# One audio tower on one core: a deeper step in the attention stage, a 32-bit pointwise convolution and a new order of work in the token stage

## The chip, the core and the metric

The kernel runs on one core of a Trainium2 chip. The time is the device time of one execution in microseconds. The kernel before took 2148.81 us (median of three runs, 2148.19 to 2150.49). One execution was also recorded by the hardware profiler. The engines of the core are PE (TensorE: matmuls, with the weight loads listed apart as PEld), DVE (VectorE), ACT (ScalarE), POOL (GpSimd) and SP (SyncE, which here only issues DMAs).

## The reference

Three stages follow each other, each on the result of the one before. All numbers are float32.

```
x [16, 64, 2048]
token stage, per batch b of 16:
  h  = conv1d(x, 7 taps, 64 -> 128 channels)              # [128, 2048]
  h  = gelu(groupnorm(h))                                 # mean and variance over channels and time
  h  = depthwise conv(h, 5 taps, stride 2) + bias         # [128, 1024]
  h  = pointwise conv(h)           # a 128 x 128 matrix product
  h  = gelu(groupnorm(h))                                 # [128, 1024]: 128 tokens of 1024 features
attention stage, on layernorm(h), 32 heads:
  q_c = rmsnorm(h @ w_qa)   [128, 384];  k_c = rmsnorm((h @ w_kva)[:, :128]);  k_r = rope(the other 64)
  scores = (q_nope . k_nope + rope(q_rope) . k_r) * 192**-0.5;  softmax over the 128 keys of the batch
  h += concat over heads(softmax @ v) @ w_o
last stage: h += layernorm(h) @ W_base.T + bias + two of eight low-rank experts per token
```

## The kernel before, in words

Nearly every matrix product is computed in 16 bits: an operand is multiplied by a power of two and stored as a high half (an ACT copy to float16) and a low half (a DVE instruction that subtracts the high half from the scaled source). Three matmuls, high by high, low by high and high by low, add up in PSUM. `dw_h` and `dw_l` are such a pair, made of `dw`, the result of the depthwise convolution.

Each engine has its own program, written out by hand, in order; engines wait for each other with semaphores. An engine whose next instruction waits does nothing else until the wait is over.

**Token stage** (`token_phase`). The function `pipeline` runs a body for i = -2 to 19. In one body, several batches are at different stages: the seven-tap convolution of batch i (four chunks of 512 columns, 12 matmuls each, L588), the depthwise convolution and the pointwise convolution of batch i-1 (`MID`), the second gelu and the layer norm of batch i-2 (`HID`), the projections of batch i-3 (`PROJ`), and the norms and transposes of the latents of batch i-4 (`TAIL`). Bodies 4 to 13 are a loop of the program, the others are written out. The order of one body, engine by engine, as far as the change touches it:

- PE: convolution chunk 0, the matmul that averages the statistics over the partitions (`stat_ps`, L642), the first four transposes of the hidden tokens, chunk 1, the other four, chunk 2, projections first half (`project(.., 0)`), chunk 3, transposes of the latents (`turn_ps<-diag,q_g`, L662), projections second half, the transposes of the rotary keys (L671), the pointwise convolution (L608 to L610).
- DVE: statistics of the pointwise result (L499), copy of the averages (L505), products with the gains, low halves, statistics of the convolution chunks (`stats1`), the five taps of the depthwise convolution (`tap`, L437 and four times L441) in three places, the latent norms (L477 to L483), the statistics for the layer norm (`bn3`, L532 and L538), low halves of the latents, low half of `dw`, low half of the rotary keys (`kr_l`).
- ACT: copies of the convolution chunks out of PSUM, high halves, first gelu (L274), second gelu (L282), high half of `dw` (L303), high half of a coming input (`x_high`), the layer-norm result `hid` (L310), high half of the rotary keys (`kr_h`, L315), the sums of squares of the projections (L323, L326).
- POOL: one chain of eleven small operations for both group norms (`group_norms`, starts at L355, ends at L362; the first gelu waits for its end), a chain of eight for the latent scales, a chain of eight for the layer norm (`layer_norm`, L384 to L387; `hid` waits for its end), the low half of a coming input (L344).

The averaging matmul of a body serves the first group norm of batch i-1 and the second of batch i-2 together, so the first gelu of a body waits for the pointwise statistics of the body before.

**Attention stage** (`attention_phase`). The work is cut into 32 rounds (8 groups of four heads, 4 quads of batches); a round has four steps j, one per batch, each for four heads. One step on PE: the scores (20 matmuls of 128 columns), the rotary queries of the next step (9 of 256 columns, `rope`), the output product of the step before (24 of 512, `outputs`), queries for the next round (9 of 512), in three of four steps a part of the weight products of a later head (float32, `products`), and the product of the probabilities with the latents of the same step (3 of 512, `av_ps`, L1141 to L1143). Between scores and latents lies the softmax: the maximum on DVE, four exponentials on ACT, normalisation on DVE, high half on ACT, low half on DVE, and a transpose of both halves by DMA that SP issues (`turn_prob`, L815). SP also issues the transpose of the rotary queries (`turn_rope`, L807). ACT and DVE then split the latents into `ot_h` and `ot_l`, which `outputs` reads. The last four rounds have no `products`, the last round no queries.

**Last stage** (`ffn_phase`): not touched.

Of the kernel before, what the change touches and what calls it, by code (L numbers as in the profile page):

```python
# [50 lines left out]
DW_S, PW_S = 2.0**5, 2.0**7  # L51
# [9 lines left out]
assert GN_SCALE == DW_S * PW_S  # L61
# [59 lines left out]
def token_phase(nc, keep, raw_loaded, x_d, wc_d, wqk_d, pw_d, rows_d, params_d, consts_d, heads_d):  # L121
# [4 lines left out]
    with ExitStack() as ctx:  # L126
# [6 lines left out]
        def sem(name):  # L133
# [8 lines left out]
        dw_h, dw_l = sb("dw_h", [P, D], F16), sb("dw_l", [P, D], F16)  # L142
# [22 lines left out]
        w_hi, w_lo = {n: sem(f"{n}_hi") for n in raw}, {n: sem(f"{n}_lo") for n in raw}  # L165
# [3 lines left out]
         st1_ready, st2_ready, stat_done, s_copied, gn_step, gelu1_done, dw_step, dw_hi, dw_lo, pw_done,  # L169
# [4 lines left out]
             "st1_ready st2_ready stat_done s_copied gn_step gelu1_done dw_step dw_hi dw_lo pw_done "  # L174
# [54 lines left out]
        def _(act):  # L229
            scales = {"wc": CW_S, "pw": PW_S, "wqk": AW_S}  # L230
# [27 lines left out]
            def body(i, p, ok):  # L258
                if isinstance(i, int) and i == 0:
                    weights_high("pw")  # L260
# [17 lines left out]
                if ok(HID):  # L278
                    b = i - HID
                    act.wait_ge(gn_step, i * GN_STEPS)  # L280
                    for hf in range(2):
                        act.activation(resid[:, bass.ds(b * D + hf * CHUNK, CHUNK)], pw_ps[hf][:, :],  # L282
                                       ACT.Gelu, bias=c12[:, 3:4], scale=c12[:, 2:3]).then_inc(gelu2_done, 1)
                if ok(TAIL):
# [4 lines left out]
                if ok(0):  # L289
                    copy_y1(i, p, 3)  # L290
# [8 lines left out]
                if ok(MID):  # L299
                    b = i - MID  # L300
# [3 lines left out]
                if ok(AHEAD) and (not isinstance(i, int) or i != -1):  # L304
                    x_high(i - AHEAD, p)
# [11 lines left out]
                if ok(PROJ):  # L317

                    b = i - PROJ
                    act.wait_ge(proj_done, b + 1)  # L320
                    need(act, rms_step, b * RMS_STEPS, B * RMS_STEPS)
                    need(act, ss_done, b * 2, 2 * B)
                    act.activation(junk[:, :], q_ps[:, 0:QR], ACT.Square, scale=UN * QR ** -0.5,  # L323
                                   accum_out=ss[:, 0:1]).then_inc(ss_done, 1)
                    act.wait_ge(ss_done, b * 2 + 1)
                    act.activation(junk[:, 0:KVR], kv_ps[:, 0:KVR], ACT.Square, scale=UN * KVR ** -0.5,  # L326
                                   accum_out=ss[:, 1:2]).then_inc(ss_done, 1)
# [79 lines left out]
        def _(dve):  # L407
# [24 lines left out]
            def tap(b, k):  # L432

                if k == 0:
                    dve.wait_ge(gelu1_done, b + 1)
                    need(dve, dw_lo, b, B)
# [48 lines left out]
            def body(i, p, ok):  # L485
# [4 lines left out]
                if isinstance(i, int) and i == 0:  # L490
                    weights_low("pw", PW_S)
# [26 lines left out]
                if ok(MID):  # L518
                    tap(i - MID, 0)
                    tap(i - MID, 1)  # L520
# [4 lines left out]
                if ok(MID):  # L525
                    tap(i - MID, 2)
# [12 lines left out]
                if ok(MID):  # L539
                    tap(i - MID, 3)  # L540
                    tap(i - MID, 4)
# [18 lines left out]
                if ok(MID):  # L560
                    b = i - MID
# [15 lines left out]
        def _(pe):  # L577
# [25 lines left out]
            def pointwise(b):  # L603
                pe.wait_ge(dw_lo, b + 1)
                need(pe, gelu2_done, b * 2, 2 * B)
                for hf in range(2):
                    sl = slice(hf * CHUNK, (hf + 1) * CHUNK)
# [892 lines left out]
```

## Time and profile before

| | us |
|---|---|
| median of three runs | 2148.81 |
| the profiled execution | 2150.39 |
| its span, first to last instruction | 2148.6 |
| token stage, to the last DVE instruction of its last body | 496.9 |
| attention stage, to its last addition into `resid` | about 1412.6 |
| last stage | about 239.1 |
| PE busy over the span | 1956.3 (91%) |
| DVE busy | 1344.1 (63%) |
| ACT busy | 792.8 (37%) |
| POOL busy | 315.4 (15%) |

The page gives shares of the span, which are averages over three stages with different limits; a stage is read by the views that take a window. In a timeline row the first number is the start in microseconds from the first instruction, the second the duration (of the group, where a count follows the x); in square brackets stands how long the engine had been idle before it, and what ended that. Ends of matmuls are modelled, so neighbouring matmuls overlap in the rows; how fast PE works is read from the distance between starts.

### The profile page before, as it was taken

To read this page: it belongs to the slowest core of one execution; us is meant where nothing else is said; L and a number is where in the kernel's file an instruction comes from. 1 tells how busy PE (TensorE), PEld (TensorE's weight loads), DVE (VectorE), ACT (ScalarE), POOL (GpSimd) and SP (SyncE) were. 2 spreads that over 40 slices of the span, in tenths; PEclk is the share of its full clock that TensorE was granted. 3 is DMA by queue.
4 is the path that set the end of the run, shared out by engine and by line. 5 is a ranking of instruction groups with operands and counts; after the bars stand their busy time and mean duration, and the time that the engine had idled before them with its cause. 6 is when DMAs were issued, how large, how long until landed. Compare 5 with 4: busy or idle time off the path is not lost. (4 is left out here: it accounts for less than half of the span.)

```text
span 2148.6 us, 42567 instructions
## 1 busy us (share of the span) xinstructions
PE 1956.3 (91%) x11826; PEld 1066.0 (50%) x11826; DVE 1344.1 (63%) x2822; ACT 792.8 (37%) x2067; POOL 315.4 (15%) x612
## 2 busy tenths in 40 slices
PE   4688888866999999999999999999999999949999
PEld 1344444443555555555555555555555555525554
DVE  3666666654666666666666666666666666655664
ACT  3344444433333333333333333333333333332221
POOL 2355555430000000000000000000000000023332
PEclk8888888978999999999999999999999999979999
DMA  4111111102222222222222222222222121142332
GB/s 136 40 40 39 39 39 39 36 1 81 55 56 55 72 54 53 53 72 54 54 53 71 55 52 54 72 54 54 54 72 54 38 38 37 38 137 70 79 86 70
DMA packets 250560, 123.82 MB, mean 58 GB/s; under 512 B 240272, under 2 KB 240528, under 8 KB 248336
## 3 DMA queue, kind: packets, MB, share of 16 engines
q1 hardware_dynamic: 246192, 94.71, 20.2%
q10 hardware_dynamic: 4320, 28.51, 3.8%
q8 instruction: 25, 0.41, 0.1%
q14 instruction: 23, 0.19, 0.0%
HBM read 56.07 MB, written 8.39 MB: 30 GB/s over the span
## 5 line engine op out<-in xcount | busy, mean ns | idle before, releaser
L1101 PE MATMUL out_ps<-m_h,ot_h 128*128 (+1 forms) x1024 | 389.7, 381 | 8.1 <-issue 3.2
L1102 PE MATMUL out_ps<-m_l,ot_h 128*128 (+1 forms) x1024 | 388.9, 380 | 0.0
L1103 PE MATMUL out_ps<-m_h,ot_l 128*128 (+1 forms) x1024 | 388.8, 380 | 0.0
L882 ACT ACTIVATE prob<-s_ps,nmx 128x128 f32<-128x128 f32 x512 | 181.3, 366 | 234.6 <-DVE nmx L975 234.6
L826 ACT ACTIVATE qp_h<-qp_ps 128x512 f16<-128x512 f32 (+1 forms) x126 | 75.2, 597 | 481.0 <-PE qp_ps L1036 481.0
L955 DVE SCALAR_TENSOR_TENSOR resid<-out_ps,resid 128x512 f32 (+1 forms) x256 | 176.2, 688 | 83.6 <-PE out_ps L1103 83.6
L905 DVE SCALAR_TENSOR_TENSOR qp_l<-qp_ps,qp_h 128x512 f16<-128x512 f32 (+1 forms) x126 | 87.2, 692 | 225.6 <-ACT qp_h L826 225.6
L1291 POOL MEMSET fpower<- 128x1 f32 x1 | 0.1, 99 | 1421.1 <-POOLq L739 1421.1
L1101 PEld LDWEIGHTS out_ps<-m_h,ot_h 128*128 128x128 f16 x1024 | 100.2, 98 | 137.6 <-issue 25.4
L1103 PEld LDWEIGHTS out_ps<-m_h,ot_l 128*128 128x128 f16 x1024 | 100.4, 98 | 113.8 <-issue 0.9
L1102 PEld LDWEIGHTS out_ps<-m_l,ot_h 128*128 128x128 f16 x1024 | 100.1, 98 | 106.4 <-issue 0.8
L905 DVE SCALAR_TENSOR_TENSOR halves<-prob,halves 128x512 f16<-128x512 f32 x128 | 88.7, 693 | 59.6 <-ACT halves L826 59.6
L826 ACT ACTIVATE halves<-prob 128x512 f16<-128x512 f32 x128 | 80.7, 631 | 85.6 <-DVE prob L981 85.6
L882 ACT ACTIVATION_READ_ACCUMULATOR prob<-s_ps,nmx 128x1 f32 x512 | 103.9, 203 | 0.0
L905 DVE SCALAR_TENSOR_TENSOR ot_l<-av_ps,ot_h 128x512 f16<-128x512 f32 x128 | 87.7, 685 | 24.8 <-ACT ot_h L826 23.9
L1036 PE MATMUL qp_ps<-qct_h,wp_h 128*128 (+1 forms) x378 | 102.8, 381 | 0.0
L1036 PE MATMUL qp_ps<-qct_h,wp_l 128*128 (+1 forms) x378 | 102.2, 379 | 0.0
L1036 PE MATMUL qp_ps<-qct_l,wp_h 128*128 (+1 forms) x378 | 102.1, 379 | 0.0
L1079 PE MATMUL s_ps<-kct_h,qp_h 128*128 (+1 forms) x512 | 93.1, 220 | 5.8 <-DVE qp_l L905 3.2
L1404 PE MATMUL fout<-wb_h,fht_h 128*128 128x512 f16 x256 | 97.3, 380 | 0.0
L1404 PE MATMUL fout<-wb_l,fht_h 128*128 128x512 f16 x256 | 97.1, 379 | 0.0
L1404 PE MATMUL fout<-wb_h,fht_l 128*128 128x512 f16 x256 | 97.0, 379 | 0.0
(246 smaller groups left out, 4130.1 us busy)
## 6 DMA issues: line engine op xcount, KB each, us to landing
wide<-heads_in ACTq DMA_DIRECT2D x30, 928.0 KB, 4.6
wide<-x_in SPq DMA_DIRECT2D x32, 512.0 KB, 6.2
tower_out<-result SPq DMA_DIRECT2D x16, 512.0 KB, 2.6
stage<-wb_in SPq DMA_DIRECT2D x8, 512.0 KB, 8.2
resid<-wqk_in SPq DMA_DIRECT2D x1, 2304.0 KB, 10.8
zt<-z SPq DMA_TRANSPOSE x128, 2.4
turned<-halves SPq DMA_TRANSPOSE x128, 3.1
wide<-heads_in SPq DMA_DIRECT2D x2, 928.0 KB, 4.6
```

Source lines behind the costliest of these rows:

```text
L826: act.activation(out, src, ACT.Copy, scale=scale).then_inc(done, 1)
L882: act.activation(prob[:, h, :], s_ps[:, h * P:(h + 1) * P], ACT.Exp, bias=nmx[:, h:h + 1], scale=EXP_SCALE, accum_out=rsum[:, h:h + 1]).th ...
L905: dve.scalar_tensor_tensor(out=out, in0=src, scalar=scale, in1=high, op0=ALU.mult, op1=ALU.subtract).then_inc(done, 1)
L955: dve.scalar_tensor_tensor(out=resid[:, at], in0=out_ps[hf][:, :], scalar=1.0 / (O_S * M_S), in1=resid[:, at], op0=ALU.mult, op1=ALU.add). ...
L1036: last = pe.matmul(bank[:, :], w[:, bass.ds(side, 1), k, j, :].rearrange("p a n -> p (a n)"), q[:, k, bass.ds(tok, CHUNK)], start=n == 0, ...
L1079: pe.matmul(out[h], q_h[h], k_h, start=h == 0, stop=False)
L1101: pe.matmul(out_ps[hf][:, :], ot_h[:, h, :], m_h[:, at], start=h == 0, stop=False)
L1102: pe.matmul(out_ps[hf][:, :], ot_h[:, h, :], m_l[:, at], start=False, stop=False)
L1103: last = pe.matmul(out_ps[hf][:, :], ot_l[:, h, :], m_h[:, at], start=False, stop=h == HEADS - 1)
L1291: pool.memset(power[:, :], -0.5).then_inc(powered, 1)
L1404: pe.matmul(out_ps[p][hf][:, :], h[p][:, k, :], w[:, k, hf * CHUNK:(hf + 1) * CHUNK], start=k == 0 and n == 0, stop=False)
```

## The change

In the token stage the pointwise convolution is one float32 matmul per half instead of three in 16 bits. Its weights are scaled once by ACT (`pw_scaled`), `dw` is read as it is, and the high half, the low half and their semaphores are gone; PE waits for the fifth tap. DVE runs the five taps one behind the other, before the third chunk statistics, the latent norms and `bn3`. PE runs the latent transposes behind the second half of the projections, then the pointwise convolution, then the transposes of the rotary keys. ACT copies the fourth chunk, then makes the high half of the coming input and the sums of squares, and then the high halves of the latents, `hid` and `kr_h`.

In the attention stage a step computes the latents and the outputs of the step before. PE runs scores, latents (j-1), rotary queries, queries, products, outputs (j-1). ACT makes `ot_h` of the step before ahead of the exponentials, DVE `ot_l` ahead of the rotation; the additions into `resid` come at the end of DVE's step. SP issues the transposes of the rotary queries of step s+1 ahead of that of the probabilities of step s.

The places in each engine's order on which the terms of the prediction rest:

DVE in the last body of the token stage that still has convolution chunks (`dw` is the depthwise result, `y_1` a copied chunk, `resid` the result of the second gelu, `bn` statistics), before:

```order
L437 TENSOR_SCALAR dw<-g,params 128x1024
L441 SCALAR_TENSOR_TENSOR dw<-g,params,dw 128x1024
L421 BN_STATS bn<-y_1 128x6
L477 RECIPROCAL rinv<-nrm 128x2
L482 TENSOR_SCALAR diag<-consts,rinv 128x128
L483 TENSOR_SCALAR k_n<-k_g,rinv 128x128
L441 SCALAR_TENSOR_TENSOR dw<-g,params,dw 128x1024
L532 BN_STATS bn<-resid 128x6 x2
L538 BN_AGGR st<-bn 128x2
L441 SCALAR_TENSOR_TENSOR dw<-g,params,dw 128x1024 x2
L421 BN_STATS bn<-y_1 128x6
```

and now:

```order
L430 TENSOR_SCALAR dw<-g,params 128x1024
L434 SCALAR_TENSOR_TENSOR dw<-g,params,dw 128x1024 x4
L414 BN_STATS bn<-y_1 128x6
L470 RECIPROCAL rinv<-nrm 128x2
L475 TENSOR_SCALAR diag<-consts,rinv 128x128
L476 TENSOR_SCALAR k_n<-k_g,rinv 128x128
L521 BN_STATS bn<-resid 128x6 x2
L527 BN_AGGR st<-bn 128x2
L414 BN_STATS bn<-y_1 128x6
```

The last two taps moved ahead of the statistics for the layer norm; POOL's layer-norm chain starts behind the `BN_AGGR` from `resid`.

PE at the end of a step of the attention stage's first round (`qp_ps` queries, `prod_ps` weight products, `av_ps` latents), before:

```order
L1036 MATMUL qp_ps<-qct_h,wp_h 128x512 x3
L1036 MATMUL qp_ps<-qct_h,wp_l 128x512 x3
L1036 MATMUL qp_ps<-qct_l,wp_h 128x512 x3
L1024 MATMUL prod_ps<-wide 128x512
L1141 MATMUL av_ps<-turned,kc_h 128x512
L1142 MATMUL av_ps<-turned,kc_l 128x512
L1143 MATMUL av_ps<-turned,kc_h 128x512
```

and now, from the end of the scores (`s_ps`) of a step of that round to the first output matmul (`out_ps`):

```order
L1075 MATMUL s_ps<-kr_l,zt 128x128
L1110 MATMUL av_ps<-turned,kc_h 128x512
L1111 MATMUL av_ps<-turned,kc_l 128x512
L1112 MATMUL av_ps<-turned,kc_h 128x512
L1041 MATMUL rope_ps<-wr_h,qct_h 128x256 x3
L1041 MATMUL rope_ps<-wr_l,qct_h 128x256 x3
L1041 MATMUL rope_ps<-wr_h,qct_l 128x256 x3
L1025 MATMUL qp_ps<-qct_h,wp_h 128x512 x3
L1025 MATMUL qp_ps<-qct_h,wp_l 128x512 x3
L1025 MATMUL qp_ps<-qct_l,wp_h 128x512 x3
L1013 MATMUL prod_ps<-wide 128x512
L1090 MATMUL out_ps<-m_h,ot_h 128x512
```

The three latent matmuls stood at the end of their own step and now stand behind the scores of the next one; the 24 output matmuls went to the end.

SP's loop over the attention steps (`z_lo` and `p_lo`: low halves written; `s_done`: scores done; `av_done`: latents done), before:

```order
L807 DMA_TRANSPOSE zt<-z 128x4x128 [waits z_lo]
L815 DMA_TRANSPOSE turned<-halves 128x8x128 [waits p_lo]
L819 UNCONDITIONAL_BRANCH
L819 ISA
L807 DMA_TRANSPOSE zt<-z 128x4x128 [waits z_lo,s_done]
L815 DMA_TRANSPOSE turned<-halves 128x8x128 [waits p_lo,av_done]
```

and now:

```order
L784 DMA_TRANSPOSE zt<-z 128x4x128 [waits z_lo]
L784 DMA_TRANSPOSE zt<-z 128x4x128 [waits z_lo,s_done]
L791 DMA_TRANSPOSE turned<-halves 128x8x128 [waits p_lo]
L796 UNCONDITIONAL_BRANCH
L796 ISA
L87 REGISTER_ALU [waits z_lo]
L784 DMA_TRANSPOSE zt<-z 128x4x128 [waits s_done]
L791 DMA_TRANSPOSE turned<-halves 128x8x128 [waits p_lo,av_done]
```

The rotary transposes run one step ahead, so that one of them is issued between two transposes of probabilities and before, not behind, that of its step.

The core of the diff:

```diff
@@ token stage, ACT
-                    weights_high("pw")
+                    act.wait_ge(w_loaded["pw"], 16)
+                    act.activation(keep["pw"][:, :], raw["pw"], ACT.Copy, scale=GN_SCALE).then_inc(pw_scaled, 1)
...
+                if ok(0):
+                    copy_y1(i, p, 3)
+                if ok(AHEAD) and (not isinstance(i, int) or i != -1):
+                    x_high(i - AHEAD, p)
+                if ok(PROJ):
+                    b = i - PROJ
+                    act.wait_ge(proj_done, b + 1)
...
                 if ok(TAIL):
                     act.wait_ge(kn_done, b + 1)
...
-                    act.wait_ge(dw_step, b * DW_TAPS + DW_TAPS)
-                    need(act, pw_done, b * 2, 2 * B)
-                    act.activation(dw_h[:, :], dw[:, :], ACT.Copy, scale=DW_S).then_inc(dw_hi, 1)
@@ token stage, DVE
                 if ok(MID):
-                    tap(i - MID, 0)
-                    tap(i - MID, 1)
+                    for k in range(DW_TAPS):
+                        tap(i - MID, k)
                 if ok(0):
                     stats1(i, p, 2)
                 if ok(TAIL):
                     latent_norms(i - TAIL)
-                if ok(MID):
-                    tap(i - MID, 2)
...
-                if ok(MID):
-                    tap(i - MID, 3)
-                    tap(i - MID, 4)
...
-                    dve.wait_ge(dw_hi, b + 1)
-                    need(dve, pw_done, b * 2, 2 * B)
-                    low(dw_l[:, :], dw[:, :], DW_S, dw_h[:, :], dw_lo)
@@ token stage, PE
             def pointwise(b):
-                pe.wait_ge(dw_lo, b + 1)
+                pe.wait_ge(dw_step, b * DW_TAPS + DW_TAPS)
...
-                    pe.matmul(pw_ps[hf][:, :], keep["pw_h"][:, :], dw_h[:, sl], start=True, stop=False)
-                    pe.matmul(pw_ps[hf][:, :], keep["pw_l"][:, :], dw_h[:, sl], start=False, stop=False)
-                    pe.matmul(pw_ps[hf][:, :], keep["pw_h"][:, :], dw_l[:, sl], start=False, stop=True
-                              ).then_inc(pw_done, 1)
+                    pe.matmul(pw_ps[hf][:, :], keep["pw"][:, :], dw[:, hf * CHUNK:(hf + 1) * CHUNK],
+                              start=True, stop=True).then_inc(pw_done, 1)
...
+                if ok(PROJ):
+                    project(i - PROJ, 1)
                 if ok(TAIL):
...
-                if ok(PROJ):
-                    project(i - PROJ, 1)
+                if ok(MID):
+                    pointwise(i - MID)
                 if ok(TAIL):
...
-                if ok(MID):
-                    pointwise(i - MID)
@@ attention stage, SP
             turn_rope(0)
+            turn_rope(1)
             turn_prob(0)
-            with sp.Fori(1, ROUNDS * QUAD) as s:
-                turn_rope(s)
+            with sp.Fori(1, ROUNDS * QUAD - 1) as s:
+                turn_rope(s + 1)
                 turn_prob(s)
+            turn_prob(ROUNDS * QUAD - 1)
@@ attention stage, ACT
+                    if before or j:
+                        latent_high(now.slot + (j - 1), not before and j == 1)
                     act.wait_ge(max_step, s * 2 + 2)
...
-                    act.wait_ge(av_done, s + 1)
-                    if before or j:
-                        act.wait_ge(out_done, s * 2)
-                    high(ot_h[:, :, :].rearrange("p h n -> p (h n)"), av_ps[:, :], O_S / (PR_S * KC_S), o_hi)
@@ attention stage, DVE
+                    if behind[0]:
+                        latent_low(now.slot + (j - 1))
                     if after or j < QUAD - 1:
                         rotate(s + 1)
...
-                    if behind[0]:
-                        add_out(*behind, 0)
-                        add_out(*behind, 1)
                     if after:
                         query_low(after, j)
                     if more and j:
                         prod_low(now.t + HEADS, now.parity, now.side * -1 + 1, now.place, j - 1, prod_ps)
-                    dve.wait_ge(o_hi, s + 1)
-                    low(ot_l[:, :, :].rearrange("p h n -> p (h n)"), av_ps[:, :], O_S / (PR_S * KC_S),
-                        ot_h[:, :, :].rearrange("p h n -> p (h n)"), o_lo)
+                    if behind[0]:
+                        add_out(*behind, 0)
+                        add_out(*behind, 1)
@@ attention stage, PE
                     scores(now, j, operands)
+                    if behind[0]:
+                        latents(*behind)
+                    if j < QUAD - 1:
+                        rope(now, j + 1)
+                    elif after:
+                        rope(after, 0)
                     if after:
                         queries(after, j)
+                    if more and j:
+                        products(now.t + HEADS, now.parity, j - 1, prod_ps, (now.t + HEADS) * 3 + (j - 1))
+                    if behind[0]:
+                        outputs(*behind)
```

## Rows read from the trace of the kernel before

**Rows 1.** Windows: stretch, length, busy of each engine (count), clock, DMA, GB/s.

```profile
119.30:391.90 272.60, 227.54 (x1201) 123.09 (x1200) 175.90 (x361) 128.56 (x200) 147.44 (x280) 0.87 0.16 38
...
569.50:1735.50 1166.00, 1150.68 (x7309) 634.06 (x7307) 765.84 (x1623) 439.65 (x1405) 0.00 (x0) 1.00 0.25 58
1735.50:1909.50 174.00, 157.70 (x992) 84.24 (x990) 101.94 (x216) 55.51 (x187) 0.00 (x0) 0.99 0.19 36
```

**Rows 2.** Timeline of ACT in the token stage: first gelu, bodies 4 and 14.

```profile
119.33 2.10 ACT L274 ACTIVATE g<-y,c 128x2048 f32<-128x2048 f32 x1 [1.16 <-POOL c L362]
...
391.94 2.10 ACT L274 ACTIVATE g<-y,c 128x2048 f32<-128x2048 f32 x1 [1.07 <-POOL c L362]
```

**Rows 3.** Timeline of all engines, 264 to 277 us: one body's end, the next's start.

```profile
263.99 2.60 DVE L441 SCALAR_TENSOR_TENSOR dw<-g,params,dw 128x1024 f32<-128x1024 f32 x2
264.34 1.02 POOL L384 TENSOR_SCALAR lv<-st 128x1 f32<-128x1 f32 x1 [4.20 <-DVE st L538]
...
268.90 0.33 PE L671 MATMUL turn_ps<-consts,kr 128*128 128x128 f32 x1 [3.33 <-DVE kct_l L412]
...
269.09 1.18 POOL L387 TENSOR_SCALAR lc<-lc 128x1 f32<-128x1 f32 x1 [0.20 <-POOL lc L386]
...
270.31 0.60 PE L608 MATMUL pw_ps<-dw_h,pw_h 128*128 128x512 f16 x1 [1.08 <-DVE dw_l L412]
...
270.49 1.24 ACT L310 ACTIVATE hid<-resid,lc,ly 128x1024 f32 x1 [0.92 <-POOL lc L387]
...
272.84 1.91 PE L588 MATMUL conv_ps<-wide,wc_h 128*128 128x512 f16 x4
...
274.44 0.22 DVE L429 SCALAR_TENSOR_TENSOR st<-st 128x1 f32<-128x1 f32 x1
...
277.16 0.28 PE L642 MATMUL stat_ps<-st,mean_mat 128*128 128x4 f32 x2
```

**Rows 4.** Timeline of POOL, 470 to 474 us: the last layer-norm chain, no taps running.

```profile
470.25 0.23 POOL L384 TENSOR_SCALAR lv<-st 128x1 f32<-128x1 f32 x1 [2.51 <-DVE st L538]
...
473.30 0.23 POOL L387 TENSOR_SCALAR lc<-lc 128x1 f32<-128x1 f32 x1 [0.20 <-POOL lc L386]
```

**Rows 5.** Timeline of PE near the start: convolution matmuls behind a gap.

```profile
22.89 1.09 PE L588 MATMUL conv_ps<-wide,wc_h 128*128 128x512 f16 x4 [2.81 <-ACT y L246]
23.78 1.91 PE L588 MATMUL conv_ps<-wide,wc_l 128*128 128x512 f16 x4
```

**Rows 6.** Timeline of PE, 504 to 506 us: two float32 matmuls of 512 columns.

```profile
504.44 1.02 PE L1024 MATMUL prod_ps<-wide 128*128 128x512 f32 x2
...
505.30 1.02 PE L1024 MATMUL s_ps<-wide 128*128 128x512 f32 x2
```

**Rows 7.** Timeline of ACT's queue: the first instruction of two rounds, two rounds apart.

```profile
828.71 0.34 ACTq L858 DMA_DIRECT2D wide<-heads_in  x1
...
915.06 0.34 ACTq L858 DMA_DIRECT2D wide<-heads_in  x1
```

**Rows 8.** Timeline, 1011 to 1022 us: one attention step and the start of the next.

```profile
1011.37 0.22 PE L1079 MATMUL s_ps<-kct_h,qp_h 128*128 x1
...
1012.20 0.69 DVE L905 SCALAR_TENSOR_TENSOR ot_l<-av_ps,ot_h 128x512 f16<-128x512 f32 x1
...
1012.49 0.49 PE L1052 MATMUL rope_ps<-wr_h,qct_h 128*128 x3
...
1013.73 0.37 ACT L882 ACTIVATE prob<-s_ps,nmx 128x128 f32<-128x128 f32 x1 [1.56 <-DVE nmx L975]
...
1017.75 1.23 SPq L815 DMA_TRANSPOSE turned<-halves  x1
...
1019.42 1.19 SPq L807 DMA_TRANSPOSE zt<-z  x1
...
1020.62 0.83 PE L1020 MATMUL prod_ps<-wide 128*128 128x128 f32 x6
...
1021.28 0.38 PE L1141 MATMUL av_ps<-turned,kc_h 128*128 128x512 f16 x1
...
1021.93 0.22 PE L1079 MATMUL s_ps<-kct_h,qp_h 128*128 x1
```

**Rows 9.** The page's list of DMA issues: median us from issue to landing.

```profile
zt<-z SPq DMA_TRANSPOSE x128, 2.4
turned<-halves SPq DMA_TRANSPOSE x128, 3.1
```

**Rows 10.** Timeline of PE in the last round: latents behind their transpose.

```profile
1871.66 0.38 PE L1141 MATMUL av_ps<-turned,kc_h 128*128 128x512 f16 x1 [1.96 <-DMA turned<-halves]
```

More of the change, by code:

```diff
@@ L869, in start, with latent_high @@
                 rope_high(0)
+            def latent_high(s, first):
+                act.wait_ge(av_done, s + 1)
+                if not first:
+                    act.wait_ge(out_done, s * 2)
+                high(ot_h[:, :, :].rearrange("p h n -> p (h n)"), av_ps[:, :], O_S / (PR_S * KC_S), o_hi)
             def body(before, now, after, more):
@@ L894, in body @@
                         prod_high(now.t + HEADS, now.parity, now.side * -1 + 1, now.place, j - 1, prod_ps, False)
-                    act.wait_ge(av_done, s + 1)
-                    if before or j:
-                        act.wait_ge(out_done, s * 2)
-                    high(ot_h[:, :, :].rearrange("p h n -> p (h n)"), av_ps[:, :], O_S / (PR_S * KC_S), o_hi)
+                if not after:
+                    latent_high(now.slot + (QUAD - 1), False)
             rounds(act, start, body)
@@ L964, in start, with latent_low @@
                 rope_low(0)
+            def latent_low(s):
+                dve.wait_ge(o_hi, s + 1)
+                low(ot_l[:, :, :].rearrange("p h n -> p (h n)"), av_ps[:, :], O_S / (PR_S * KC_S),
+                    ot_h[:, :, :].rearrange("p h n -> p (h n)"), o_lo)
             def body(before, now, after, more):
@@ L968, in body @@
                     s = now.slot + j
+                    behind = (now, j - 1) if j else (before, QUAD - 1)
                     dve.wait_ge(s_done, s + 1)
@@ L983, in body @@
                                       ).then_inc(norm_step, 1)
-                    behind = (now, j - 1) if j else (before, QUAD - 1)
                     if after or j < QUAD - 1:
@@ L1112, in start, with latents @@
                 rope(Round(pe, 0), 0)
+            def latents(r, j):
+                if not r.known or r.t or j:
+                    pe.wait_ge(o_lo, r.slot + j)
+                at = bass.ds(r.tok + j * P, P)
+                probs_h, probs_l = (turned[:, at, :].rearrange("p h n -> p (h n)")
+                                    for at in (slice(0, HEADS), slice(HEADS, 2 * HEADS)))
+                pe.wait_ge(p_turned, r.slot * 16 + (16 * j + 16))
+                pe.matmul(av_ps[:, :], kc_h[:, at], probs_h, start=True, stop=False)
+                pe.matmul(av_ps[:, :], kc_l[:, at], probs_h, start=False, stop=False)
+                pe.matmul(av_ps[:, :], kc_h[:, at], probs_l, start=False, stop=True).then_inc(av_done, 1)
             def body(before, now, after, more):
@@ L1116, in body @@
                 for j in range(QUAD):
[L1117 removed]
+                    behind = (now, j - 1) if j else (before, QUAD - 1)
                     scores(now, j, operands)
[L1119 to L1128 removed]
+                    if behind[0]:
[4 more added lines that the diff above has]
+                        rope(after, 0)
                     if after:
                         queries(after, j)
+                    if more and j:
+                        products(now.t + HEADS, now.parity, j - 1, prod_ps, (now.t + HEADS) * 3 + (j - 1))
+                    if behind[0]:
+                        outputs(*behind)
                     if j < QUAD - 1:
                         operands = score_operands(now, j + 1)
[L1133 to L1143 removed]
                 if not after:
+                    latents(now, QUAD - 1)
                     outputs(now, QUAD - 1)
```

78 lines of the change are left out of this document (19 added, 59 removed).

## The prediction

> **What bounds the kernel now.** I first read the windows, then the timelines behind them. From the first gelu of body 4 to that of body 14 lie ten equal periods, (391.94 - 119.33) / 10 = 27.26 us each [rows 2]. In that stretch PE is busy for 227.54 of 272.60 us at a granted clock of 0.87, so it both waits and works part of the time at 1.2 GHz [rows 1]. The steady attention stage is another picture: 1150.68 of 1166.00 us at clock 1.00 [rows 1]; only gaps can be won there. Its last four rounds leave 174.00 - 157.70 = 16.3 us idle [rows 1].
>
> In the token stage the timeline shows what closes the circle from one first gelu to the next [rows 3]: taps (dw), the low half of dw on DVE, the pointwise product, convolution chunk 0, the averaging matmul, POOL's group norm, gelu. PE has been idle for 3.33 us before the rotary-key transposes and 1.08 us more before the pointwise product, and then works at 1.2 GHz: the six pointwise matmuls take (272.84 - 270.31) / 6 = 0.42 us each, and the averaging matmul, behind chunk 0, starts only at 277.16, though its input st2 was ready at 274.44 + 0.22 = 274.66 [rows 3]. In the same stretch POOL's layer-norm chain runs from 264.34 to 269.09 + 1.18 = 270.27, that is 5.93 us [rows 3]; the last such chain of the stage, with no taps beside it, takes from 470.25 to 473.30 + 0.23 = 473.53, 3.28 us [rows 4].
>
> A step of the attention stage waits at its own end: the latents need a transpose that SP issues late, with 3.1 us to landing [rows 8, 9], so they are queued behind everything else, and DVE's and ACT's split of the latents then stands between steps.
>
> **The change, token stage.** I follow the circle and count differences; before and now both end at the same gelu (2.10 us [rows 2]).
> - The split of dw goes, one ACT copy and one DVE instruction per body, and with it what made the pointwise product late. Two float32 matmuls stand for six in 16 bits. Their price at 2.4 GHz is 505.30 - 504.44 = 0.86 us [rows 6], 1.72 for both, against 6 x 0.42 = 2.52 at 1.2 GHz now; at 1.2 GHz the new pair would take 3.44. They now wait only for the taps, which end before PE comes to them, so I put them off the circle. The scaling copy of the weights takes the place of a high half of the same size: nothing.
> - With the split gone, the circle closes through the layer norm: bn3, POOL's chain, hid, the high and low half of the rotary keys, the statistics st2, the averaging matmul. The last two taps now stand ahead of bn3, +2.60 us [rows 3].
> - No tap runs beside the layer-norm chain any more. Its first instruction took 1.02 us beside a tap and takes 0.23 alone [rows 3, 4]. By the whole chain, 3.28 for 5.93: -2.65 us.
> - The averaging matmul follows its input instead of chunk 0: 274.66 + 0.1 for 277.16, -2.40 us.
>
> The Trainium skill gives a rule for this: by "SBUF — State Buffer", section "Who interferes with whom", a DVE instruction with two inputs in SBUF contends with a GpSimd instruction that reads SBUF, and the other one blocks for the whole instruction. The trace agrees (1.02 for 0.23 [rows 3, 4]). The rule also speaks against the change, since five taps in a row leave POOL's latent-scale chain only the gaps between taps; by it four instructions wait up to one tap each, 4 x 1.3 = 5.2 us, about as long as the four taps last, and the sum would be 0 to 3 us worse over the loop.
>
> Sum of the circle: 2.60 - 2.65 - 2.40 = -2.45 us. Against it stands a cost that no row shows directly. PE will now find chunk 0 done and st2 missing: it is idle for about 274.8 - 272.0 = 2.8 us, an estimate from [rows 3]. Behind a gap of 2.81 us near the start four convolution matmuls took 1.91 us, the half-clock duration of [rows 3], after a first 1.09 [rows 5]. So chunk 1 may run at 1.2 GHz; that is some 1.7 us of PE, of which only the part that delays a copy ahead of the gelu on ACT's queue counts, 0 to 0.85. I take 0.4: -2.05 per period, ten periods -20.5. The bounds are -2.45 and -1.0 (gap and half clock fully on the circle): -10 to -25. The first bodies (1 to 3) and last bodies (14 to 16 and the end) have other limits, a coming input's split on POOL and the shorter queues; from their shorter share of the same circle I estimate -1 and -0.5 for one body, bounds 0 and -2.05: -4 together, 0 to -8. Token stage: -24, range -10 to -33.
>
> **The change, attention stage.** A round lasts (915.06 - 828.71) / 2 = 43.17 us [rows 7]. A step without a product takes 1021.93 - 1011.37 - 0.66 = 9.90 us, where 0.66 is the product from 1020.62 to 1021.28 [rows 8]. Four steps, and products of 0.66 and twice 0.86 [rows 6] in three of them, make 39.60 + 2.38 = 41.98; so 1.19 us of a round are waits. These are of three kinds: outputs waiting for the split of the latents, latents for the transpose, scores for DVE. The work on PE is the same after the change, instruction by instruction; only the waits can go.
>
> What is late next? Now the transpose of step s is needed behind the scores of step s+1, at 9.90 + (1012.49 - 1011.37) = 11.0 us from its own scores' start [rows 8]. On DVE the split ot_l (0.69) moves into the softmax, ahead of the rotation, and delays its tail by that: SP's issue moves from 1017.75 - 1011.37 = 6.38 to 7.07, and with 3.1 to landing to 10.2 [rows 8, 9]. On SP it may also have to follow the rotary transpose, which occupies SP for 1.19 [rows 8]: 11.4 at worst, if that issue starts just ahead. I take 10.4, 0.6 before it is needed. The exponentials now stand behind ot_h on ACT: 1.12 for the scores, 0.65 for the latents (1021.28 to 1021.93) and about 0.7 for the copy make 2.5, against 1013.73 - 1011.37 = 2.36 today [rows 8]; so that cost is inside the 0.69. The outputs at the end of a step have both halves long before. The additions into resid come last on DVE; the next maximum waits behind them for at most a few tenths, and DVE is busy for 765.84 of 1166.00 us only [rows 1].
>
> Of the 1.19 us I let 0.9 of it go: 27 rounds with products, 27 x 1.19 x 0.9 = -29, bounds 0 and -32 (more than the waits can't be won, since PE's work stays; a loss here is a rival below). In the last four rounds 16.3 us are idle, the larger part the latents' wait for their transpose (1.96 us in the last round [rows 10]); about half stays, since without products the step is shorter by the same transpose: -8, bounds 0 and -12. Attention: -37, range 0 to -44. The last stage is not touched.
>
> Sum: 2150.39 - 24 - 37 = 2089 against the profiled execution, whose span is 2148.6 and whose time lies 1.6 us above the median of the runs; against that median 2088.
>
> **The rivals.** (A) The layer-norm chain stays slow: chunk statistics, low halves and bn3's neighbours run beside POOL as the taps did. Then 2.65 falls out of the sum in whole, for a period of 27.26 - 2.05 + 2.65 = 27.86 and 2148.8 + 6 - 4 - 37 = 2114, or in half, for 26.5 and 2101; I put it at 2108. For it: DVE is busy on two-input work all through the body. Against it: [rows 4] has low halves on DVE too.
>
> (B) The rotary transpose, now issued just ahead, holds that of the probabilities back by its own transfer. Today it is issued 1.67 us behind the other one (1019.42 - 1017.75) and lands after 2.4 [rows 8, 9]. A delay of 1.5 puts the landing at about 11.9, 0.9 later than needed; the latents, ot_h and the exponentials form a ring with it, so each step is 10.8 us, as 43.17 / 4 is today. Then attention gives nothing but the tail, 2148.8 - 24 - 6 = 2119.
>
> (C) The same ring on the other side: if the rotary transfer takes its whole 2.4 us first, the landing is 7.07 + 2.4 + 3.1 = 12.6, the ring is 12.6 - 1.1 = 11.5, and 124 steps lose 0.7 each: +87 - 24, 2212 us. It turns the change slower from a ring of 10.8 + 24 / 124 = 11.0 us. Against it: the two run within 1.67 us of each other today with medians of 2.4 and 3.1.
>
> (D) PE's clock does not come back in the token stage behind its new gap. PE's work of a period at full clock is 227.54 x 0.87 / 10 = 19.8 us [rows 1]; all of it at 1.2 GHz would be 39.6, +12.3 on the period: 2148.8 + 123 - 37 = 2235. Against it: today two gaps of 3.33 and 1.08 precede chunk 0, and the clock is still 0.87 on the whole.
>
> The Trainium skill names this loop in "TensorE: Matmul & The Clock Gate", section "HAM oscillation — how this bites in real kernels": a loop whose waits let the clock fall pays for it in each turn. The 0.42 us matmuls of [rows 3] show that this kernel pays today already.
>
> **How the numbers follow.** Forecast 0.66; A 0.13; B 0.10; C 0.05; D 0.03; nothing moves 0.03. The likeliest case has a range of its own of 2066 to 2106 (token -10 to -33, attention -30 to -44 with the middle favoured). Taking in A and B the range is 2060 to 2122. A run of this kernel can be told from no change from about 0.2%, 4.3 us: faster 0.66 + 0.13 + 0.10 = 0.89, the same 0.03, slower 0.08.
>
> **What would show it.** Ten periods of the first gelu of about 25.2 us; POOL's chain L384 to L387 (by its new lines) at 3.3 us; the averaging matmul right behind st2 and not behind chunk 0; two pointwise matmuls of 0.86 us; rounds of 42.1 us; few waits of PE for the transposes of the probabilities. It would be wrong if the granted clock of the token stretch falls below 0.87, if the chain still takes 5 us, or if PE waits at the latents in every step.

## The result and the profile after

The changed kernel takes 2131.48 us (median of four runs, 2130.34 to 2133.41), 0.9915 of the kernel before (2149.65 us, median of four runs beside it), with a 95% interval of 0.9903 to 0.9927: 18 us less, where 2088 us, 62 less, was forecast, and outside the range of 2060 to 2122. The profiled execution takes 2130.34 us with a span of 2128.6.

The two stages went different ways. The first matmul of the attention stage, kernel before, then after (start, duration, engine, line, operation, tiles):

```profile
497.21 1.19 PE L1020 MATMUL prod_ps<-wide 128*128 128x128 f32 x4 [0.96 <-PEq L126]
```

```profile
472.04 1.19 PE L1009 MATMUL prod_ps<-wide 128*128 128x128 f32 x4 [0.96 <-PEq L124]
```

The token stage gave 25.2 us. The span fell by 20.0 only, so what follows got 5.2 us longer, where -37 was forecast for it.

The token stage came out near its forecast of -24. The first gelu of bodies 4 and 14 (as [rows 2]) and the windows of that stretch and of the steady attention stage (length, busy PE, PEld, DVE, ACT, POOL, clock, DMA share, GB/s, as [rows 1]):

```profile
115.27 2.10 ACT L272 ACTIVATE g<-y,c 128x2048 f32<-128x2048 f32 x1 [0.84 <-POOL c L355]
...
369.05 2.10 ACT L272 ACTIVATE g<-y,c 128x2048 f32<-128x2048 f32 x1 [1.07 <-POOL c L355]
```

```profile
115.27:369.05 253.78, 216.74 (x1182) 119.97 (x1181) 165.82 (x353) 117.08 (x191) 121.52 (x280) 0.96 0.18 42
...
575.00:1680.00 1105.00, 1068.42 (x6798) 594.68 (x6796) 703.05 (x1512) 396.94 (x1313) 0.00 (x0) 1.00 0.26 57
```

A token period is 25.38 us instead of 27.26. In the attention stage, where PE was busy for 98.7% of its time [rows 1], it now is for 1068.42 of 1105.00, 96.7%: it waits more than before, and the wait can be read at one place of each round. All DMA issues and PE's waits from 1021 to 1032 us, the last step of one round and the start of the next (ACTq and SPq are DMA issues):

```profile
1021.76 1.19 SPq L784 DMA_TRANSPOSE zt<-z  x1
...
1022.04 0.35 ACTq L836 DMA_DIRECT2D wide<-heads_in  x1
...
1023.14 1.23 SPq L791 DMA_TRANSPOSE turned<-halves  x1
...
1027.71 0.23 PE L1074 MATMUL s_ps<-kr_h,zt 128*128 x1 [0.24 <-DMA zt<-z]
...
1028.54 0.39 PE L1110 MATMUL av_ps<-turned,kc_h 128*128 128x512 f16 x1 [0.20 <-DMA turned<-halves]
...
1031.18 0.81 PE L1025 MATMUL qp_ps<-qct_h,wp_h 128*128 x3 [0.77 <-issue]
...
1109.67 0.35 ACTq L836 DMA_DIRECT2D wide<-heads_in  x1
```

ACT issues the load of a coming head's weights between the two transposes. The last row is the same load two rounds later: (1109.67 - 1022.04) / 2 = 43.82 us a round, against 43.17 [rows 7]. The list of DMA issues (last number: us to landing), first of 1021 to 1025 us, with the load, then of the next step, 1033 to 1039 us, without one:

```profile
wide<-heads_in ACTq DMA_DIRECT2D x1, 928.0 KB, 5.4
zt<-z SPq DMA_TRANSPOSE x1, 5.9
turned<-halves SPq DMA_TRANSPOSE x1, 5.3
```

```profile
zt<-z SPq DMA_TRANSPOSE x1, 2.4
turned<-halves SPq DMA_TRANSPOSE x1, 3.0
```

Beside the load the rotary transpose needs 5.9 us instead of 2.4 and that of the probabilities 5.3 instead of 3.0. Both are late for the scores and the latents of the next step, once in four steps. PE's waits from 575 to 1680 us in the changed kernel (total, times, longest):

```profile
PE qp_ps L1025 <- issue: 20.0, 26, 0.8
PE s_ps L1074 <- DMA zt<-z: 11.8, 24, 2.2
PE av_ps L1110 <- DMA turned<-halves: 3.9, 19, 0.2
```

The largest of them is not a wait for a transpose but time ahead of the queries in which PE waited for nothing that the profile shows. In the kernel before the load of a round was alone (ACTq and SPq rows around the first load of [rows 7]):

```profile
825.55 1.19 SPq L807 DMA_TRANSPOSE zt<-z  x1
...
834.74 1.23 SPq L815 DMA_TRANSPOSE turned<-halves  x1
```

Issued at 828.71 [rows 7], it had 6.0 us until the next transpose. What ACT did ahead of the load shows why its time moved (`qp_h`, `m_h` and `ot_h` are the high halves of queries, products and latents), before, then after:

```profile
826.61 0.60 ACT L826 ACTIVATE qp_h<-qp_ps 128x512 f16<-128x512 f32 x1 [3.65 <-PE qp_ps L1036]
827.56 0.60 ACT L826 ACTIVATE m_h<-prod_ps 128x512 f32 x1 [0.36 <-PE prod_ps L1024]
828.11 0.60 ACT L826 ACTIVATE ot_h<-av_ps 128x512 f16<-128x512 f32 x1
```

```profile
1021.76 0.58 ACT L804 ACTIVATE qp_h<-qp_ps 128x512 f16<-128x512 f32 x1
1022.24 0.59 ACT L804 ACTIVATE m_h<-prod_ps 128x512 f32 x1
1029.48 0.60 ACT L804 ACTIVATE ot_h<-av_ps 128x512 f16<-128x512 f32 x1 [6.65 <-PE av_ps L1112]
```

Before, PE came to queries and products only behind its outputs, so ACT's copies of them were late, and the load behind them too. Now PE does both ahead of the outputs and the copies come right behind the softmax. The one copy that still waits, `ot_h`, has been moved behind the load.

The rounds that load nothing show what the new order is worth by itself. The first maximum of the last three rounds, after and then before:

```profile
1767.34 0.69 DVE L960 TENSOR_REDUCE mx<-s_ps 128x4 f32<-128x512 f32 x1 [0.32 <-PE s_ps L1075]
...
1846.30 0.69 DVE L960 TENSOR_REDUCE mx<-s_ps 128x4 f32<-128x512 f32 x1 [0.32 <-PE s_ps L1075]
```

```profile
1778.63 0.69 DVE L970 TENSOR_REDUCE mx<-s_ps 128x4 f32<-128x512 f32 x1 [1.34 <-PE s_ps L1086]
...
1863.58 0.69 DVE L970 TENSOR_REDUCE mx<-s_ps 128x4 f32<-128x512 f32 x1 [0.58 <-PE s_ps L1086]
```

Two such rounds take 78.96 us for 84.95: 3.0 us less each.

### The profile page after: what moved, and what is told of

The parts are those of the page before. It is cut to its first block and busy times, and to the rows that moved or that the text cites. A ratio compares the mean times of both kernels' runs of the same rounds, so it can differ in the third digit from the quotient of the medians.

```text
span 2128.6 us, 42839 instructions
## 1 busy us (share of the span) xinstructions
PE 1938.4 (91%) x11794; PEld 1066.4 (50%) x11794; DVE 1314.6 (62%) x2805; ACT 757.9 (36%) x2051; POOL 279.4 (13%) x612
## 5 line engine op out<-in xcount | busy, mean ns | idle before, releaser
L804 ACT ACTIVATE ot_h<-av_ps 128x512 f16<-128x512 f32 x128 | 76.4, 597 | 762.5 <-PE av_ps L1112 762.5
L960 DVE TENSOR_REDUCE mx<-s_ps 128x4 f32<-128x512 f32 x128 | 88.5, 692 | 63.9 <-PE s_ps L1075 63.9
L868 ACT ACTIVATION_READ_ACCUMULATOR prob<-s_ps,nmx 128x1 f32 x512 | 109.0, 213 | 0.0
```

Of the source, the lines that this page charges most:

```text
L804: act.activation(out, src, ACT.Copy, scale=scale).then_inc(done, 1)
L868: act.activation(prob[:, h, :], s_ps[:, h * P:(h + 1) * P], ACT.Exp, bias=nmx[:, h:h + 1], scale=EXP_SCALE, accum_out=rsum[:, h:h + 1]).th ...
L960: dve.tensor_reduce(mx[:, :], s_ps[:, :].rearrange("p (h n) -> p h n", h=HEADS), AX.X, ALU.max).then_inc(max_step, 1)
```

## The experiments

Theory L: the load moved. On ACT the high half of the latents stood at the end of a step, ahead of the load that opens the next round. The change took it into the next step, behind the load, and brought the copies of queries and products forward; so the load is now issued beside the two transposes and slows them down. Rivals: R, the rotary transpose just ahead holds that of the probabilities back in every step; Q, PE's own issue time behind the moved waits. Each time is a median of 4 to 12 runs; the kernel before ran beside them, with medians of 2149.96 to 2152.22 us in the three groups of runs, so two kernels of different groups can be compared to within about 3 us.

**The load behind the landed transpose.**

```diff
                     act.wait_ge(wr_lo, now.t + HEADS)
+                    if before:
+                        act.wait_ge(p_turned, now.slot * 16)
                     load(now.t + HEADS + 1, 1 - now.parity)
```

Expected: 

> The changed kernel; ACT's load of a coming head (928 KB, once a round) waits until the round's first transpose of probabilities has landed, so that it no longer runs beside the two transposes. Theory L (the load, which the change moved ahead of the latents' split, holds back both transposes once a round): the rotary transpose of that step lands in 2.4 us again instead of 5.9, rounds go from 43.9 us to about 42.0, 27 rounds, 2131 - 51 = 2080 us. Rival R (the rotary transpose issued just ahead holds that of the probabilities back in every step): no change, 2131. Rival Q (PE's own issue time behind the moved waits): the 0.8 us ahead of the queries once a round stays, half of the gain, about 2106.

Measured 2095.62 us, 0.9738 (0.9724 to 0.9751) of the kernel before: 36 us less than the changed kernel. The new wait is for the last transpose of the round before, and the load follows its landing at 1011.92. The next transposes land in 2.4 and 3.0 us; two loads lie 1096.74 - 1011.92 = 84.82 apart, 42.41 a round. R falls. Of 51 us, 15 did not come. Three are the token stage's, which took longer in this profile (first maximum of the attention stage at 504.68 for 501.55); 0.42 x 27 = 11 are in the rounds, 42.4 and not 42.0. One wait of PE has outlived the load, ahead of the queries of a round's first step, and there Q has a part. Over 575 to 1680 us it fell from 20.0 to 9.6 us (second view, total of that window), so about half of it came with the load; in which way was not tested:

```profile
1057.92 0.81 PE L1027 MATMUL qp_ps<-qct_h,wp_h 128*128 x3 [0.55 <-issue]
```

```profile
PE qp_ps L1027 <- issue: 9.6, 26, 0.6
```

**The load with few bytes**, in the rounds.

```diff
-                act.dma_start(raws[p][:, 0:RAW], heads_d[...]
+                act.dma_start(raws[p][:, 0:64], heads_d[...]
```

Expected: 

> The changed kernel; the loads of the rounds move only the first 64 columns of a head, the other columns keep an earlier head's values. Place and waits of the load as in the changed kernel. Theory L: with hardly any bytes the transposes land on time, rounds of about 42.0, 2080 us, the same as with the load moved. Rival R: 2131. If it is the place of the load's issue on ACT and not its bytes that costs: 2131 too, while the moved load gains.

Measured 2092.67 us, 0.9729 (0.9715 to 0.9742). This kernel leaves out most of the weights it should load and serves for its time alone. With the issue in its place and 32 KB for 928 the rounds are 42.4 us as well (1092.07 - 1007.28 = 84.79 for two): the bytes cost, not the issue.

**The cost put into the kernel before.**

```diff
@@ kernel before, ACT: the load leaves the start of the round
                     high(p_h, prob[:, :, :].rearrange("p h n -> p (h n)"), PR_S, p_hi)
+                    if more and j == 0 and (not now.known or now.t + HEADS + 1 < NH):
+                        act.wait_ge(prod_done, now.t * 3 + 3 * HEADS)
+                        act.wait_ge(wr_lo, now.t + HEADS)
+                        load(now.t + HEADS + 1, 1 - now.parity)
```

Expected: 

> The kernel before; the load of a round is issued in the round's first step behind the high half of the probabilities, so that it runs beside the two transposes. Theory L: the landing of the probabilities goes from 3.1 to 5.5 us in one step of four, PE waits about 2 us more per round: 27 x 2 = 54, about 2204 us. Rivals R and Q: nothing moves, 2149.

Measured 2206.89 us, 1.0261 (1.0247 to 1.0275), 56 us more, as theory L had it. From 575 to 1680 us PE waits 49.7 us at the latents, where the kernel before waited 6.2. One such wait, and the landings of 1024 to 1031 us:

```profile
1075.05 0.39 PE L1141 MATMUL av_ps<-turned,kc_h 128*128 128x512 f16 x1 [2.02 <-DMA turned<-halves]
```

```profile
wide<-heads_in ACTq DMA_DIRECT2D x1, 928.0 KB, 4.9
turned<-halves SPq DMA_TRANSPOSE x1, 4.8
zt<-z SPq DMA_TRANSPOSE x1, 3.5
```

**The order of load and split undone.**

```diff
                     if before or j:
                         latent_high(now.slot + (j - 1), not before and j == 1)
+                    if more and not j and (not now.known or now.t + HEADS + 1 < NH):
+                        act.wait_ge(prod_done, now.t * 3 + 3 * HEADS)
+                        act.wait_ge(wr_lo, now.t + HEADS)
+                        load(now.t + HEADS + 1, 1 - now.parity)
```

Expected: 

> The changed kernel; the load stands right behind the high half of the latents in the round's first step, the place among the instructions that it had before, without any added wait. Theory L: it is issued about 2.6 us into the step and lands some 5 us later, at 7.7, beside the two transposes (issued at 6.0 and 7.2), which then land up to 1.5 us late with 0.7 of slack: 0 to 1 us per round over the kernel with the load behind the landed transpose, 2096 to 2120 us. Rival R or Q alone: 2131.

Measured 2093.73 us, 0.9736 (0.9722 to 0.9749). Four lines moved behind the split, with no new wait, win as much as the gated load: in the new order the split's wait for the latents is enough to keep the load clear. I had feared a collision with the next transposes; the rows show 3.6 us from the load to the first of them (its landing 4.5 us, theirs 2.4 and 3.0):

```profile
1014.01 0.35 ACTq L836 DMA_DIRECT2D wide<-heads_in  x1
1017.60 1.19 SPq L784 DMA_TRANSPOSE zt<-z  x1
1018.98 1.23 SPq L791 DMA_TRANSPOSE turned<-halves  x1
```

**The two parts apart.** The changed token stage with the attention stage of before, and the reverse.

Expected: 

> The changed token stage with the attention stage of the kernel before. From the traces the token stage gave 25 us (first matmul of the attention stage at 472.0 for 497.2) and the attention stage lost about 5: 2149.6 - 25 = 2124 us if the stages don't touch each other; 2131 if the loss lies in the handover between them.

Expected: 

> The token stage of the kernel before with the changed attention stage. If the two parts add up, the changed attention stage by itself is a loss: the changed kernel is at 2131.5, the changed token stage alone at 2128.1, so +3.4 on 2150.7, about 2154 us. If the attention stage gains by itself and loses only behind the changed token stage: below 2148.

Measured 2128.12 us, 0.9888 (0.9872 to 0.9903), and 2157.82 us, 1.0021 (1.0013 to 1.003). The token part alone is 22.6 us faster than the kernel before beside it, the attention part alone 5.6 us slower by the medians and 4.5 by the ratio. Together that is 17 to 18 us less, where 18.2 was measured: they add up.

**Two taps behind the statistics again.**

```diff
-                    for k in range(DW_TAPS):
+                    for k in range(DW_TAPS - 2):
                         tap(i - MID, k)
...
                     dve.bn_aggr(st3[:, :], bn3[:, :, :]).then_inc(bn3_step, 1)
+                if ok(MID):
+                    tap(i - MID, 3)
+                    tap(i - MID, 4)
```

Expected: 

> The changed kernel; the last two taps stand behind the statistics for the layer norm again, so that they run beside POOL's layer-norm chain. By the steps of the prediction the circle loses 2.60 us of taps ahead of the statistics and gets 2.5 us in the chain (5.9 for 3.4): a period as before, 25.4 us, 2131 us within 5. If the taps beside it cost the chain nothing, the period falls by 2.6: about 2105 us.

Measured 2119.94 us, 0.9853 (0.9839 to 0.9868): 11.5 us faster than the changed kernel by the medians (13 by the ratios), between the two answers. The first and the last rows of POOL's layer-norm chain, in the changed kernel and in this one:

```profile
253.52 0.23 POOL L377 TENSOR_SCALAR lv<-st 128x1 f32<-128x1 f32 x1 [5.98 <-DVE st L527]
253.93 0.57 POOL L112 TENSOR_TENSOR ly<-lv,half 128x1 f32<-128x1 f32 x1 [0.18 <-POOL lv L377]
...
256.70 0.23 POOL L380 TENSOR_SCALAR lc<-lc 128x1 f32<-128x1 f32 x1 [0.20 <-POOL lc L379]
```

```profile
247.82 1.02 POOL L377 TENSOR_SCALAR lv<-st 128x1 f32<-128x1 f32 x1 [3.34 <-DVE st L527]
249.02 1.48 POOL L112 TENSOR_TENSOR ly<-lv,half 128x1 f32<-128x1 f32 x1 [0.18 <-POOL lv L377]
...
252.57 0.23 POOL L380 TENSOR_SCALAR lc<-lc 128x1 f32<-128x1 f32 x1 [0.20 <-POOL lc L379]
```

3.41 us alone, 4.98 beside the taps. Two taps hold up two of the eight instructions, 1.57 us, and cost 2.60 where they stand ahead: five in a row lose about 1 us per period. The ten periods took 242.2 us, for 253.8 to 258.0 in five profiles with the token code of the changed kernel, 1.2 to 1.6 us each. The rest of the 5.93 us of before [rows 3], 0.95, is the chain's last instruction: L387 took 1.18 us [rows 3] beside the low half of `dw` and takes 0.23 here. That low half in the kernel before:

```profile
268.96 1.22 DVE L412 SCALAR_TENSOR_TENSOR dw_l<-dw,dw_h 128x1024 f16<-128x1024 f32 x1
```

**The product in 16 bits in the new order.** The two splits and the six matmuls come back, high half behind that of the coming input on ACT, low half behind the statistics of the convolution on DVE.

Expected: 

> The changed kernel with the pointwise product in 16 bits again (six matmuls, high half of dw on ACT behind that of the coming input, low half on DVE behind the statistics of the convolution), in the changed order. By the prediction the product is off the circle, which closes through the layer norm: 2131 to 2136 us. If the 32-bit product by itself made the gain of the token stage: back to about 2150.

Measured 2150.30 us, 0.9992 (0.9984 to 1.0001): as slow as the kernel before. My expectation falls; in this order the split is on the path again. PE waits 3.04 us for the low half, and 31.0 us in the ten periods together:

```profile
243.56 0.39 PE L602 MATMUL pw_ps<-dw_h,pw_h 128*128 128x512 f16 x1 [3.04 <-DVE dw_l L411]
```

The ten periods are 26.06 us each (first gelus at 124.93 and 385.52), 0.68 more than in the changed kernel, 7 of the 19 us lost; the other 12 lie in the first bodies and at the end. The attention stage is the changed one and still loses its 5 us, so the token stage keeps about 5 of its gain: the first maximum comes at 520.62, for 525.95 before and 501.55 in the changed kernel. Without the 32-bit product the new order thus gives 5 of 24 us. What the product would give in the old order was not run.

**Keys ahead of the hidden tokens, coming input ahead of the layer norm**, on top of the first experiment.

```diff
@@ token stage, ACT: kr_h ahead of hid; POOL:
+                if ok(AHEAD) and (not isinstance(i, int) or i >= 0):
+                    x_low(i - AHEAD, p)
                 if ok(HID):
                     layer_norm(i - HID)
-                if ok(AHEAD) and (not isinstance(i, int) or i >= 0):
-                    x_low(i - AHEAD, p)
```

Expected: 

> The changed kernel with the load behind the landed transpose (as in the experiment before), and in the token stage ACT's high half of the rotary keys ahead of the layer-norm result, POOL's low half of the coming input ahead of the layer-norm chain. The statistics st2 then come about 2.3 us earlier: a period of about 23.0 for 25.4 us, 2095.6 - 24 - 3 = about 2069 us. If POOL's 3.8 us holds the layer norm up, half of it: about 2082 us.

Measured 2104.90 us, 0.9767 (0.975 to 0.9784), 9 us slower than without it by the medians, 6 by the ratios. Neither theory had this: POOL's 4.07 us met an instruction of DVE that takes 0.29 us otherwise (POOL, then DVE):

```profile
236.52 4.07 POOL L337 TENSOR_TENSOR x_l<-wide 128x2054 f16<-128x2054 f32 x1 [3.28 <-ACT wide L237]
...
236.81 3.85 DVE L475 TENSOR_SCALAR diag<-consts,rinv 128x128 f32<-128x128 f32 x1 [0.32 <-DVE rinv L470]
```

and the latent transposes waited for it. It was the rule and not one body: in the ten periods this instruction took 3.63 us in the median, PE waited 36.3 us for the one behind it, and the periods took 270.0 us for 257.6 in the first experiment. What the keys' new place did by itself was not run.

**The two findings together, and PE's registers early.** The first of these has the gated load and the two taps behind; the second also computes the positions of the next round on PE ahead of the scores:

```diff
             def body(before, now, after, more):
+                if after:
+                    after.slot, after.group, after.side, after.tok
                 operands = score_operands(now, 0)
```

Expected: 

> The changed kernel with the load behind the landed transpose (first experiment) and the last two taps behind the statistics for the layer norm (sixth). If the two causes lie in different stages they add up: 2095.6 - 11.5 = 2084 us. If the token stage's gain is eaten at the handover: 2095.

Expected: 

> The kernel of the run before in this call, and PE computes the next round's position registers ahead of the round's first scores instead of between the rotary queries and the queries. If the 0.4 to 0.7 us of issue time that PE still spends there in the first step of a round is these registers (rival Q): 27 x 0.5 = 13 us less, 2071 us. If it is something else: 2084.

Measured 2079.54 us, 0.9674 (0.9661 to 0.9687), and 2072.58 us, 0.9638 (0.9625 to 0.9651). The causes add up (the two taps give 14 to 16 us here), and the registers give 7 of the 13 us expected: the issue time ahead of the queries was 9.7 us from 575 to 1680 us, 0.22 to 0.55 us a round, and falls to 0.3. Rounds are now 42.0 us and PE has no wait left in the steady stage (window of the last kernel, as above):

```profile
575.00:1600.00 1025.00, 1024.60 (x6586) 575.00 (x6584) 681.10 (x1467) 385.05 (x1274) 0.00 (x0) 1.00 0.26 60
```

This version beats both kernels: 77 us under the one before, 59 under the changed one.

## Why the prediction was wrong

**The step that failed** is the attention stage's "Of the 1.19 us I let 0.9 of it go", the -29 us of the 27 rounds with products. It asked what is late next and counted SP's two transposes, DVE's queue and the exponentials on ACT, and took 3.1 us to landing for given, with 0.6 us to spare. It did not follow ACT's queue to its other instruction there, the load. Queries and products had moved ahead of the outputs on PE, and `latent_high` behind the load on ACT; with both, nothing held the load back until the transposes were under way. It came beside them instead of 6.0 us ahead of the next, they took 5.9 and 5.3 us to landing, and a round got 0.65 us longer instead of 1.07 shorter. None of the rivals held this. With the load apart from the transposes (two ways of moving it, or few bytes) the rounds fall from 43.82 to 42.4; from the first maximum (at 525.95, 501.55 and 503.59) to the end of the span (2148.6, 2128.6 and 2092.8) the kernel before needs 1622.7 us, the changed one 1627.1 and the one with the order undone 1589.2, a gain of 33.5 where 37 was forecast. So the term was nearly right for a kernel whose load stays clear of the transposes.

**What held.** The landings' margin in the other steps: with the load away PE waits for a transpose only once, 0.2 us, from 575 to 1680 us, so rivals B and C, the rotary transpose ahead, are refuted. The clean round of 41.98 worked out from [rows 8] is what the last version reaches, 42.01. In the last rounds, where 2 us of each were to come (8 over four), 3.0 came.

**The token stage** was forecast at -24 and measured at -25.2 in this profile and -22.6 over runs. The period was 25.38 for 25.2. The layer-norm chain took 3.41 us for 3.28, so rival A is refuted, and the pointwise product waited for nothing. The averaging matmul does wait for st2 behind chunk 0:

```profile
261.46 0.38 PE L620 MATMUL stat_ps<-st,mean_mat 128*128 128x4 f32 x2 [2.57 <-DVE st L422]
```

2.57 us, 2.8 foreseen. Inside that sum one term had the wrong reason: only 1.57 of the 2.65 us of the layer-norm chain were the taps', and the rest went with the split. The two taps put ahead were booked as almost nothing (2.60 against 2.65) and lose at least 1 us per period. That the total came out all the same is luck in part, since the split went too. That the 32-bit product is off the circle was right, but that it would be so in 16 bits too, as I expected of the experiment, was not. The cost feared for POOL's latent-scale chain is there but off the path: its last three instructions took 0.70, 1.15 and 1.12 us in one body, and it ended at 247.53, where DVE came to it at 250.65.

**The clock**, rival D, did not decide: 0.96 for 0.87 before. But it goes with the noise of this stage. Three periods of the first experiment's kernel (the window's clock stands third from the end), with the same token code:

```profile
192.04:219.32 27.28, 23.73 (x120) 12.85 (x119) 16.67 (x35) 11.65 (x21) 10.67 (x29) 0.87 0.17 38
...
270.56:295.91 25.35, 22.11 (x120) 12.44 (x119) 16.60 (x35) 11.65 (x21) 11.03 (x28) 0.93 0.19 41
347.13:372.01 24.88, 21.73 (x125) 12.08 (x124) 17.49 (x39) 11.77 (x20) 11.85 (x27) 1.00 0.11 38
```

The lower the granted clock of a period, so the more of it PE runs at 1.2 GHz, the longer it is, up to 2.4 us. The prediction took 0.4 us for this, 0.85 at most. The ten periods took 253.8 to 258.0 us in five profiles of this token code. What sets the number of slow periods was not tested, and stays open.

## What to carry to other kernels

When instructions that wait are moved, on their engine or on the one they wait for, look at what stood behind them: the waits were also the timer of that. A DMA issue is the one to look for first, since it costs next to nothing on its own engine and shows only in the landing of somebody else's transfer; compare landings step by step (5.9 for 2.4 us once in four), for a median over all steps hides them (2.4 us before and after). And when a chain is slow beside another engine's work, measure each neighbour's share before moving one of them onto the path.

## What the runs showed of the hardware

Beside a load of 928 KB on one DMA queue, small transposes on another landed in 5.9 us instead of 2.4 and in 5.3 instead of 3.0, and the load itself took 5.4 us instead of 4.6. A DVE instruction of 0.29 us with one tensor input took 3.85 us beside a POOL instruction of 4.07 us; the Trainium skill, "SBUF — State Buffer", section "Who interferes with whom", says that `tensor_scalar` can enter modes that contend with GpSimd when its operands meet certain conditions, and this trace fits; which mode this instruction was in no run shows. PE's address registers, computed between a wait and the next matmuls, showed as 0.22 to 0.55 us of issue time per round until they were computed earlier.
